# Turning the tiles of three passes on VectorE and by DMA instead of on TensorE

## The chip, the cores and the metric

The kernel runs on one core of a Trainium2 chip. The metric is the device time of one execution in microseconds. All arithmetic is in float32; the large products are made of three products each, of a high and a low part of both factors (`three`, lines 559 to 566).

## What is computed

The input x has 4 sequences of 512 tokens of width 512 (2048 tokens). Six steps are added to it in turn:

```
x = x + 0.5 * ffn0(layernorm(x))      ffn0: silu(x W1^T) * (x W3^T), Walsh-Hadamard, W2^T; hidden 2048
x = x + attention(layernorm(x))       normalised again, gamma and beta, causal softmax, plus residual
x = x + 0.5 * ffn0(layernorm(x))
x = x + 0.5 * ffn1(layernorm(x))      gate and up with ternary weights and scales, down; hidden 1408
x = x + state(layernorm(x))           tanh(x B^T) C^T + D * x; state 256
x = x + 0.5 * ffn1(layernorm(x))
```

## The kernel before

The instructions of each engine are written out by hand in program order; semaphores join the engines. x stays in SBUF, 16 tiles of 128 tokens. Each of the four ffn steps is done in two passes, one for each half of the tokens (a pair of sequences, 8 tiles): passes 0 and 1 are the first ffn0, 2 and 3 the second, 4 and 5 the first ffn1, 6 and 7 the second. Attention lies between passes 1 and 2, the state step between 5 and 6.

A pass is a loop over slots, one for each block of 128 hidden units: 16 slots of an ffn0 pass ("A") and 11 of an ffn1 pass ("B"). The up products of a slot are seven products on 128x512 tiles (p1, p5, p6, p2, then p7, p3, p4), a Strassen-Winograd scheme that works on 2x2 blocks: the half of the tokens and the half of the hidden units. PE's order in a slot is the first half (p1, p5, p6, p2), four down tiles of earlier slots (`down`, each into a bank of a ring of three PSUM banks; a bank is free again when VectorE has added it into x, line 2107), then the turns of that slot, then the second half (p7, p3, p4).

The products need the normalised tokens of a pass turned, with the features in the partitions. They are prepared ahead: pass 0 turns the tiles for pass 1, pass 2 for 3, 3 for 4, 4 for 5, 5 for the state step and 6 for 7; those of passes 0, 2 and 6 come from the opening, from attention and from the state step. Slots `norms` (5 to 8 in pass 0, 3 to 6 in passes 2 and 3): ScalarE normalises two tiles (`norm_pair`, line 1452) into `xn`. Slots `turn_slots`, one later: PE turns each of the two tiles by four transposes of 128x128 against an identity matrix (`turn_tiles`, `turn`, lines 997 and 855) into a bank of the same ring, and ScalarE copies the bank to `xs` (`turn_out`, line 1300). In the third-last and the second-last slot of a pass VectorE forms the sums of the scheme from `xs` (`sums`, line 2053), and in the last slot the high and low parts `xc_hi` and `xc_lo` for the next pass are made (`convert`, lines 1308 and 2072).

In a slot VectorE's order is `seed_z` (line 2136), the low part of the next weight block (pass 0 only, line 2091), the four adds, statistics in some slots, `sum_c22` (line 2145), the two gatings, then `hid_low` of token half 1 and of half 0 (line 2133), and in pass 0 the four sums of a raw weight block (line 2080). ScalarE makes the high parts in `hid_high` (line 1444), for half 0 after `seed_y` of the next slot.

All transfers are issued by SyncE's queue (SP) in program order. In pass 0 it stores the prepared weights (`w13_out`, `w2_out`) and fetches raw ones two blocks ahead. In later passes it loads, in the iteration of slot s, the up weights of slot s+1 (`w13_load`, line 579), which wait for p4 of slot s-1, and a down block (`w2_load`). There are two buffers of up weights and four of down weights.

## Time and profile before

| | |
|---|---|
| time, median of 3 runs | 1707.72 us (1706.44 to 1708.61) |
| profiled execution, span | 1703.6 us |
| PE busy | 1694.7 us, 99% |
| VectorE busy | 1154.4 us, 68% |
| ScalarE busy | 830.3 us, 49% |
| TensorE's granted clock, mean | 0.999 |
| moved by DMA | 344.56 MB, mean 202 GB/s |

The profile is of one execution, and its span runs from the first to the last instruction; no time of its own is given beside the span, so it stands next to the median of the timed runs, which is 4.1 us longer. Busy time of PE is the union of pipelined matmuls, so 99% says that it is never long without one.

### The profile page before, as it was taken

How to read it: one execution, taken by the hardware profiler on the slowest of the kernel's cores; microseconds unless marked ns; L12 is line 12 of the kernel's file. 1: busy time of each engine (PE TensorE's matmuls, PEld its weight loads, DVE VectorE, ACT ScalarE, POOL GpSimd, SP SyncE). 2: the span in 40 equal slices, each digit the busy share in tenths (PEclk: the TensorE clock that was granted, in tenths of full speed). 3: DMA queues.
4: the chain of work that ended last, by engine and by line, in shares of the span. 5: the costliest groups of instructions: out<-in, count | busy, mean ns of one | idle time of the engine just before them, and what ended most of it. 6: DMA issues, size and time to landing. Idle time of an engine off the chain costs nothing.

```text
span 1703.6 us, 21742 instructions
## 1 busy us (share of the span) xinstructions
PE 1694.7 (99%) x7707; PEld 1401.8 (82%) x7707; DVE 1154.4 (68%) x1808; ACT 830.3 (49%) x1359; POOL 125.5 (7%) x185
## 2 busy tenths in 40 slices
PE   9999999999999999999999999999999999999998
PEld 7788888888888888888888888888888888888887
DVE  8888678677775555754446554447768869877866
ACT  5745444465575543434223333224556556655644
POOL 1000000000012220000000000000000143200001
PEclk9999999999999999999999999999999999999999
DMA  9776665699985000253444433444666763366765
GB/s 317 266 310 247 229 258 211 236 377 369 369 333 207 1 0 1 87 191 126 153 167 167 167 142 136 167 167 146 232 215 211 273 222 112 113 242 234 257 221 213
DMA packets 97341, 344.56 MB, mean 202 GB/s; under 512 B 10192, under 2 KB 25424, under 8 KB 91856
## 3 DMA queue, kind: packets, MB, share of 16 engines
q1 hardware_dynamic: 97232, 343.14, 55.0%
q8 instruction: 65, 1.06, 0.2%
q14 instruction: 44, 0.36, 0.1%
HBM read 261.83 MB, written 81.26 MB: 201 GB/s over the span
## 4 chain that ended last, share of the span: by engine, by line
PE 94%; DVE 3%; DMA 1%; SPq 1%; issue 1%; ACT 0%; DVEq 0%; ACTq 0%
PE psum L561 35%; PE psum L563 30%; PE psum L565 27%; PE psum L857 2%; DMA x<-in_w2a 1%; SPq L705 1%; DVE xc_lo L2074 0%; DMA flat<-in_w3a 0%; DMA w<-w_kept 0%; PE psum L1134 0%; DVE att_lo L2043 0%; DVE fw_lo L2037 0%; SPq L664 0%; DVE x L2020 0%; DVE x L2123 0%
## 5 line engine op out<-in xcount | busy, mean ns | idle before, releaser
L561 PE MATMUL psum<-xc_hi,w 128*128 128x512 f32 x1544 | 604.6, 392 | 0.5 <-DVE psum L2143 0.3
L563 PE MATMUL psum<-xc_lo,w 128*128 128x512 f32 x1544 | 600.9, 389 | 0.0
L565 PE MATMUL psum<-xc_hi,w 128*128 128x512 f32 x928 | 361.3, 389 | 0.0
L561 PEld LDWEIGHTS psum<-xc_hi,w 128*128 128x128 f32 x1544 | 289.8, 188 | 64.4 <-DVE psum L2143 1.6
L563 PEld LDWEIGHTS psum<-xc_lo,w 128*128 128x128 f32 x1544 | 289.9, 188 | 58.8
L561 PE MATMUL psum<-w,hid 128*128 128x512 f32 x864 | 337.5, 391 | 0.0
L565 PE MATMUL psum<-w,hid 128*128 128x512 f32 x864 | 336.4, 389 | 0.0
L2107 DVE TENSOR_TENSOR x<-psum,x 128x512 f32<-128x512 f32 x256 | 173.0, 687 | 148.3 <-PE psum L565 147.7
L563 PE MATMUL psum<-w,hid 128*128 128x512 f32 x544 | 211.7, 389 | 0.0
L565 PEld LDWEIGHTS psum<-xc_hi,w 128*128 128x128 f32 x928 | 174.2, 188 | 36.7
L2131 DVE TENSOR_TENSOR hid<-sg,hid 128x512 fp32r<-128x512 f32 x212 | 144.3, 691 | 85.2 <-ACT hid L1450 83.3
L561 PEld LDWEIGHTS psum<-w,hid 128*128 128x128 f32 x864 | 162.2, 188 | 36.1 <-DVE x L2107 2.7
L565 PEld LDWEIGHTS psum<-w,hid 128*128 128x128 f32 x864 | 162.2, 188 | 33.9
L1480 ACT ACTIVATE psum<-psum 128x512 f32<-128x512 f32 x108 | 62.9, 582 | 237.6 <-PE psum L565 172.4
L1450 ACT ACTIVATE hid<-sg 128x512 fp32r<-128x512 f32 x204 | 125.6, 627 | 105.1 <-DVE sg L2156 51.9
L2147 DVE TENSOR_TENSOR sg<-psum,sg 128x512 f32<-128x512 f32 x104 | 71.6, 688 | 91.1 <-ACT psum L1480 90.7
L563 PEld LDWEIGHTS psum<-w,hid 128*128 128x128 f32 x544 | 102.2, 188 | 20.4
L2143 DVE TENSOR_TENSOR psum<-psum,sg 128x512 f32<-128x512 f32 x104 | 72.2, 694 | 43.8 <-PE psum L565 36.9
L1423 ACT ACTIVATE psum<-psum 128x512 f32<-128x512 f32 x108 | 62.8, 581 | 79.9 <-PE psum L565 54.7
L1884 POOL TENSOR_SCALAR var_eps<-meanvar 128x4 f32<-128x4 f32 x24 | 7.0, 290 | 1242.1 <-DVE meanvar L1988 865.1
L1472 ACT ACTIVATE sg<-psum 128x512 f32<-128x512 f32 x64 | 38.0, 593 | 89.2 <-PE psum L565 89.2
L1298 ACT ACTIVATE xn<-x,shift,rstd 128x512 f32<-128x512 f32 x88 | 65.7, 807 | 13.0 <-POOL shift L1887 9.9
(177 smaller groups left out, 2030.1 us busy)
## 6 DMA issues: line engine op xcount, KB each, us to landing
w<-w_kept SPq DMA_DIRECT2D x93, 896.0 KB, 6.6
w<-w_kept SPq DMA_DIRECT2D x130, 512.0 KB, 7.1
w<-w_kept SPq DMA_DIRECT2D x57, 640.0 KB, 4.4
w_kept<-w SPq DMA_DIRECT2D x16, 1792.0 KB, 7.3
w<-w_kept SPq DMA_DIRECT2D x93, 256.0 KB, 4.5
w_kept<-prep SPq DMA_DIRECT2D x12, 1792.0 KB, 7.6
w_kept<-w SPq DMA_DIRECT2D x16, 512.0 KB, 6.3
w_kept<-prep SPq DMA_DIRECT2D x12, 512.0 KB, 8.9
```

What stands on the lines that cost most here:

```text
L561: pe.matmul(out, a_hi, b_hi, start=start, stop=False, skip_group_check=onto)
L563: last = pe.matmul(out, a_hi, b_lo, start=False, stop=stop and zero == "a", skip_group_check=onto)
L565: last = pe.matmul(out, a_lo, b_hi, start=False, stop=stop, skip_group_check=onto)
L1298: return copy(out, x[:, i, :], AF.Identity, bias=shift[:, i:i + 1], scale=rstd[:, i:i + 1])
L1423: copy(bank(BY), bank(BX), AF.Copy).then_inc(y_seeded, 1)
L1450: copy(hid_of(u, c)[:, 0, :], own(u) if c else sg[:, 0, :], AF.Copy).then_inc(hid_hi_ready, 1)
L1472: copy(sg[:, 0, :], bank(BX), AF.Silu, scale=gate_scale(ps, s)).then_inc(c11_read, 1)
L1480: copy(bank(BW), bank(BY), AF.Copy).then_inc(w_seeded, 1)
L2107: tt(at_x, b, at_x, ALU.add).then_inc(added, 1)
L2131: tt(h[:, 1, :], source, h[:, 0, :], ALU.subtract).then_inc(hid_ready, 1)
L2143: tt(bank(BZ), bank(BY), own(u), ALU.add).then_inc(z_seeded, 1)
L2147: tt(own(u), bank(BY), own(u), ALU.add).then_inc(c22_ready, 1)
```

## The change

The turns of passes 0, 2 and 3 leave TensorE. In each `norms` slot of these passes ScalarE normalises two tiles into `xn[:, 0:2]`, each after VectorE has read the tile before in that buffer. VectorE then transposes each tile in 32x32 blocks into `swap` (a new use of the second half of `xn`), where the two tiles of a pair lie interleaved token by token. Four stores, one for each group of 32 partitions, write the pair to DRAM so that the blocks come in their new order, SP waits for them, and four loads bring it to `xs`. A piece that is contiguous in DRAM has 256 bytes in the stores and 1 KB in the loads. The tokens of passes 1, 3 and 4 then lie in pairs; `hid_high` and `hid_low` read them with a step of two and write the plain order. The other turns (for passes 0, 2, 5, 6, 7, the state step and attention) stay on TensorE. The blocks of `xs` are renumbered, and waits that counted turned tiles are counted anew.

```diff
@@ -75,6 +75,9 @@
 NORMS = {4: (3, 4, 5, 6), 5: (4, 5, 6, 7), 6: (4, 4, 5, 6), 7: ()}
 CONVERSIONS = {no: (3, 0, 2, 1, 4, 5, 6) if no == BEFORE_S else tuple(range(7)) for no in range(len(PASSES))}
+SWAPPED = (0, 2, 3)
+BLOCK = 32
+LANDED = 16 * 4
 FIRST_CONVERSION = {5: 6, 6: 5, 7: 6}
 TURNS = {4: (4, 5, 6, 7), 5: (5, 6, 7, 8), 6: (4, 5, 6, 7), 7: ()}
...
@@ -155,7 +163,7 @@
                         n = 2 * TURNED_EARLY.index(s) + j
                         self.bank["t", n] = b
                         ps.turns[s].append((n, n))
-            elif no < len(PASSES) - 1 and s in ps.turn_slots:
+            elif no < len(PASSES) - 1 and no not in SWAPPED and s in ps.turn_slots:
                 for j in range(2):
                     self.use(("n", self.turn), 3)
                     ps.turns[s].append((self.turn, 2 * ps.turn_slots.index(s) + j))
...
@@ -226,6 +235,7 @@
     w2_raw = nc.dram_tensor("w2_scratch", [HA // P, P, D], F32).ap()
     w13_kept = nc.dram_tensor("w13_kept", [W13_BASE["S"] + 1, P, 2 * 7 * 2 * P], F32).ap()
     w2_kept = nc.dram_tensor("w2_kept", [W2_BASE["S"] + 2, P, 2 * D], F32).ap()
+    turn_scratch = nc.dram_tensor("turn_scratch", [BLOCK, P // BLOCK, KD, P // BLOCK, 2 * BLOCK], F32).ap()
     mix_raw = nc.dram_tensor("mix_raw", [2, P, KD * D], F32).ap()
     mix_kept = nc.dram_tensor("mix_kept", [2, P, 2, KD * D], F32).ap()
...
@@ -254,9 +264,10 @@
         w2 = at("w2", [P, 4, 2, D], F32R, "w2")
         hid = at("hid", [P, 5, 2, TOK], F32R, "hid")
-        hid_more = [at(f"hid_more{i}", [P, 2, TOK], F32R, "xs", (4 + 8 * i) * KIB) for i in range(2)]
+        hid_more = [at(f"hid_more{i}", [P, 2, TOK], F32R, "xs", (8 + 4 * i) * KIB) for i in range(2)]
         sg = at("sg", [P, 3, TOK], F32, "sg")
         xn = at("xn", [P, 4, D], F32, "xn")
+        swap = at("swap", [P, P // BLOCK, KD, BLOCK, 2], F32, "xn", 4 * KIB)
         flat = at("flat", [P, 12, 2 * P], F32, "sp")
...
@@ -443,9 +457,31 @@
             return conv_base(no) + CONVERSIONS[no].index(m) + 1
-        def turns_before(no):
-            return PT * (no + 1 + (no >= BEFORE_S))
+        def all_turned(no):
+            if no - 1 in SWAPPED:
+                return turn_in[no - 1], PT // 2 * LANDED
+            return turned, PT * {0: 1, BEFORE_T: 2, BEFORE_S - 1: 3, BEFORE_S: 5, BEFORE_S + 1: 6}[no]
+        def swaps_before(ps):
+            return PT * SWAPPED.index(ps.no)
+        def paired(no):
+            return no - 1 in SWAPPED
+        def of_unit(u):
+            return next(ps.no for ps in passes if ps.u0 <= u < ps.u0 + ps.n)
+        def in_pairs(tile, no):
+            return tile.rearrange("p (h t i) -> p h i t", h=2, i=2) if paired(no) else tile
+        def by_tile(tile, no):
+            return tile.rearrange("p (h i t) -> p h i t", h=2, i=2) if paired(no) else tile
         def hid_of(u, c):
...
@@ -480,7 +516,7 @@
         def xs_cols(tile):
             c, i = tile // TT, tile % TT
-            return xs[:, c:c + 3:2, :, i * P:(i + 1) * P]
+            return xs[:, 2 * c:2 * c + 2, :, i * P:(i + 1) * P]
         def bank_tiles(b):
             return bank(b).rearrange("p (h k t) -> p h k t", h=2, k=2)
...
@@ -524,11 +560,11 @@
                 return score_ready, CH * TT
             return t_full, filled["v", CH - 1, 1]
-        sources = [xs[:, 0, :, :], xn[:, 0:2, :], xs[:, 4, :, :], xs[:, 2, :, :], xs[:, 1, :, :], xs[:, 3, :, :],
+        sources = [xs[:, 0, :, :], xn[:, 0:2, :], xs[:, 4, :, :], xs[:, 1, :, :], xs[:, 2, :, :], xs[:, 3, :, :],
                    xn[:, 2:4, :]]
         freeing = [p1_done, p5_done, p6_done, p2_done, p7_done, p3_done, p4_done]
-        s_sources = [xs[:, 0, :, :], xs[:, 2, :, :], xs[:, 1, :, :], xs[:, 3, :, :]]
+        s_sources = [xs[:, n, :, :] for n in range(4)]
         def s_blocks(c):
...
@@ -686,7 +722,10 @@
             def mix_raw_load(r):
                 sp.wait_ge(mix_stored[r // 2], 16)
-                sp.wait_ge(turn_ready, PT if r < 2 else 2 * PT)
+                if r < 2:
+                    sp.wait_ge(turn_ready, PT)
+                else:
+                    sp.wait_ge(*all_turned(1))
                 if r:
                     sp.wait_ge(mix_split_kept, 16 * r)
                 sp.dma_start(mix_in_raw[:, :, :].rearrange("p k d -> p (k d)"),
...
@@ -704,6 +743,23 @@
                     sp.wait_ge(fw_out, 4 * s + j + 1)
                     sp.dma_start(w2_raw[4 * j:4 * j + 4, :, s * P:(s + 1) * P].rearrange("b p d -> p b d"),
                                  stage_of(s, j).rearrange("p (b d) -> p b d", b=4)).then_inc(scratch_done[j], 16)
+            def turn_load(ps, k):
+                c, cols = k // 2, slice(k % 2 * 2 * P, (k % 2 + 1) * 2 * P)
+                sp.wait_ge(swapped, swaps_before(ps) + 2 * k + 2)
+                if k:
+                    sp.wait_ge(turn_in[ps.no], k * LANDED)
+                elif SWAPPED.index(ps.no):
+                    sp.wait_ge(*all_turned(SWAPPED[SWAPPED.index(ps.no) - 1] + 1))
+                for a in range(P // BLOCK):
+                    sp.dma_start(turn_scratch[:, :, :, a, :].rearrange("i b k t -> i (b k) t"),
+                                 swap[a * BLOCK:(a + 1) * BLOCK, :, :, :, :].rearrange("p b k j i -> p (b k) (j i)")
+                                 ).then_inc(turn_stored[ps.no], 16)
+                sp.wait_ge(turn_stored[ps.no], (k + 1) * LANDED)
+                for b in range(P // BLOCK):
+                    sp.dma_start(xs[b * BLOCK:(b + 1) * BLOCK, 2 * c:2 * c + 2, :, cols].rearrange("p h k t -> p (h k) t"),
+                                 turn_scratch[:, b, :, :, :].rearrange("i k a t -> i k (a t)")).then_inc(turn_in[ps.no], 16)
             rows_in(0)
             sp.dma_start(had_raw[:, :], t["hadamard"]).then_inc(had_in, 16)
...
@@ -753,6 +809,8 @@
                 w2_out(s)
                 if s in MIX_IN:
                     mix_split_out(MIX_IN.index(s))
+                if s in passes[0].norms:
+                    turn_load(passes[0], passes[0].norms.index(s))
                 if s + 1 in MIX_IN:
                     mix_raw_load(MIX_IN.index(s + 1))
...
@@ -785,6 +843,8 @@
                         w2_load(ps.w2_0 + s, W2_BASE[ps.kind] + s)
                     if early and not late_low:
                         w13_low_load(ps.v0 + s + 1, W13_BASE[ps.kind] + s + 1)
+                    if ps.no in SWAPPED and s in ps.norms:
+                        turn_load(ps, ps.norms.index(s))
                     if ps.no == 1:
                         if s == 0:
                             sp.dma_start(half_down_s[:, :], t["down_s"]).then_inc(hds_in, 16)
...
@@ -1446,11 +1506,21 @@
                 if u == 0:
                     act.wait_ge(mix_stored[1], 16)
                 if plan.hid_set[u, c] >= 5:
-                    act.wait_ge(xc_ready, conv_base(next(ps.no for ps in passes if ps.u0 <= u < ps.u0 + ps.n)) + 7)
-                copy(hid_of(u, c)[:, 0, :], own(u) if c else sg[:, 0, :], AF.Copy).then_inc(hid_hi_ready, 1)
+                    act.wait_ge(xc_ready, conv_base(of_unit(u)) + 7)
+                no = of_unit(u)
+                copy(by_tile(hid_of(u, c)[:, 0, :], no), in_pairs(own(u) if c else sg[:, 0, :], no),
+                     AF.Copy).then_inc(hid_hi_ready, 1)
             def norm_pair(ps, k):
+                if ps.no in SWAPPED:
+                    for tile in (2 * k, 2 * k + 1):
+                        if k:
+                            act.wait_ge(swapped, swaps_before(ps) + tile - 1)
+                        else:
+                            act.wait_ge(xc_ready, conv_base(ps.no) + 7)
+                        normalise(norm_event(ps) + tile // TT, tile % TT, xn[:, tile % 2, :]).then_inc(xn_ready, 1)
+                    return
                 first = [n for r in ps.turns for n, _ in r][0]
                 for tile in (2 * k, 2 * k + 1):
                     if tile >= TT:
@@ -1531,11 +1601,6 @@
                     if ps.no == 0 and s == ps.norms[0]:
                         act.wait_ge(mix_split_kept, 32)
                     norm_pair(ps, ps.norms.index(s))
-                if ps.no != BEFORE_T - 1:
-                    for n, tile in ps.turns[s]:
-                        if tile == 0:
-                            act.wait_ge(xc_ready, conv_base(ps.no) + 7)
-                        turn_out(n, tile, plan.bank["n", n])
                 seed_w(u)
                 if last and following:
                     convert(following, 2)
...
@@ -2052,9 +2117,9 @@
             def sums(ps, step):
-                b11, b12, b21, b22, t2 = (xs[:, n, :, :] for n in range(5))
+                b11, b21, b12, b22, t2 = (xs[:, n, :, :] for n in range(5))
                 if step == 0:
-                    dve.wait_ge(turned, turns_before(ps.no))
+                    dve.wait_ge(*all_turned(ps.no))
                     tt(b12, b22, b12, ALU.subtract).then_inc(sums_ready, 1)
                 elif step == 1:
                     dve.wait_ge(sums_ready, 4 * ps.no + 1)
...
@@ -2077,6 +2142,15 @@
                 dve.wait_ge(xc_hi_ready, conv_base(BEFORE_S) - 4 + m + 1)
                 tt(xc_lo[:, m, :, :], s_sources[m], xc_hi[:, m, :, :], ALU.subtract).then_inc(xc_ready, 1)
+            def swap_pair(ps, k):
+                for j in range(2):
+                    dve.wait_ge(xn_ready, plan.norm_base[ps.no] + 2 * k + j + 1)
+                    if k:
+                        dve.wait_ge(turn_stored[ps.no], k * LANDED)
+                    nc.vector.transpose(swap[:, :, :, :, j], xn[:, j, :].rearrange("p (k b t) -> p b k t", k=KD, b=P // BLOCK)
+                                        ).then_inc(swapped, 1)
             def w13_sums(n):
                 dve.wait_ge(*raw_landed(n))
...
@@ -2126,12 +2200,13 @@
                 for _, i, d in ps.downs[ps.n][TT * half:TT * (half + 1)]:
                     finish_tile(ps, i, d)
-            def low(key, h, source):
+            def low(key, h, source, no):
                 dve.wait_ge(hid_hi_ready, plan.lo_no[key])
-                tt(h[:, 1, :], source, h[:, 0, :], ALU.subtract).then_inc(hid_ready, 1)
+                tt(by_tile(h[:, 1, :], no), in_pairs(source, no), by_tile(h[:, 0, :], no),
+                   ALU.subtract).then_inc(hid_ready, 1)
             def hid_low(u, c):
-                low((u, c), hid_of(u, c), own(u) if c else sg[:, 0, :])
+                low((u, c), hid_of(u, c), own(u) if c else sg[:, 0, :], of_unit(u))
             def seed_z(u):
                 dve.wait_ge(p6_done, u + 1)
...
@@ -2238,6 +2313,9 @@
                 if following and s in (ps.n - 3, ps.n - 2):
                     for step in range(2):
                         sums(following, 2 * (s - ps.n + 3) + step)
+                swapping = ps.no in SWAPPED and s in ps.norms
+                if swapping and ps.no:
+                    swap_pair(ps, ps.norms.index(s))
                 if not last:
                     sum_c22(u)
                     if preparing and s == 1:
@@ -2247,6 +2325,8 @@
                         w2_split(0)
                         w2_split(1)
                     hid_low(u, 1)
+                    if swapping and ps.no == 0:
+                        swap_pair(ps, ps.norms.index(s))
                     hid_low(u, 0)
                 if ps.no == 0 and s != 1 and s + 2 < UNITS["A"]:
                     w13_sums(s + 2)
```

## Rows read from the trace of the kernel before

**Rows 1.** The page, parts 1 and 4: engines over the span; chain that ended last.

```profile
PE 1694.7 (99%) x7707; PEld 1401.8 (82%) x7707; DVE 1154.4 (68%) x1808; ACT 830.3 (49%) x1359; POOL 125.5 (7%) x185
...
PE 94%; DVE 3%; DMA 1%; SPq 1%; issue 1%; ACT 0%; DVEq 0%; ACTq 0%
```

**Rows 2.** Waits of PE (total us, times, longest), first and last of four.

```profile
PE psum L1233 <- POOL warm L1861: 1.3, 1, 1.3
...
PE psum L561 <- DVE psum L2143: 0.3, 1, 0.3
```

**Rows 3.** Timeline of ScalarE in pass 0: start, length, one copy per slot.

```profile
126.06 0.58 ACT L1480 ACTIVATE psum<-psum 128x512 f32<-128x512 f32 x1 [4.76 <-PE psum L565]
...
141.07 0.58 ACT L1480 ACTIVATE psum<-psum 128x512 f32<-128x512 f32 x1 [0.17 <-PE psum L565]
...
156.99 0.58 ACT L1480 ACTIVATE psum<-psum 128x512 f32<-128x512 f32 x1 [0.68 <-PE psum L565]
```

**Rows 4.** The same timeline in pass 2.

```profile
740.81 0.58 ACT L1480 ACTIVATE psum<-psum 128x512 f32<-128x512 f32 x1 [6.20 <-PE psum L565]
...
755.77 0.58 ACT L1480 ACTIVATE psum<-psum 128x512 f32<-128x512 f32 x1 [4.80 <-PE psum L565]
...
771.62 0.58 ACT L1480 ACTIVATE psum<-psum 128x512 f32<-128x512 f32 x1 [0.67 <-PE psum L565]
```

**Rows 5.** Groups by form: busy us, mean ns of one, idle before.

```profile
L1985 DVE BATCH_NORM_STATS2 stats<-x 128x6 f32<-128x512 f32 x72 | 45.2, 678 | 0.1
...
L857 PE MATMUL psum<-ident,xn 128*128 128x128 f32 x320 | 41.6, 273 | 0.2
...
L2074 DVE TENSOR_TENSOR xc_lo<-xn,xc_hi 128x1024 fp32r<-128x1024 f32 x16 | 19.5, 1217 | 1.8 <-ACT xc_hi L1329 1.8
...
L2009 DVE TENSOR_SCALAR y<-x,rstd,shift 128x512 f32<-128x512 f32 x4 | 1.9, 542 | 1.5 <-POOL shift L1887 1.5
```

**Rows 6.** Timeline of VectorE in pass 0, from one slot into the next.

```profile
160.41 0.69 DVE L2131 TENSOR_TENSOR hid<-sg,hid 128x512 fp32r<-128x512 f32 x1
162.24 0.69 DVE L2131 TENSOR_TENSOR hid<-sg,hid 128x512 fp32r<-128x512 f32 x1 [1.15 <-ACT hid L1450]
...
164.10 0.42 DVE L2089 TENSOR_TENSOR flat<-flat 128x256 f32<-128x256 f32 x1
...
166.29 2.02 DVE L2094 TENSOR_TENSOR w<-flat,w 128x1792 fp32r<-128x1792 f32 x1 [1.16 <-ACT w L1352]
```

**Rows 7.** Timeline of ScalarE in the same slot.

```profile
164.55 1.70 ACT L1352 ACTIVATE w<-flat 128x1792 fp32r<-128x1792 f32 x1 [1.51 <-DVE flat L2089]
```

**Rows 8.** Timeline of the weight loads (PEld) in the same slot.

```profile
168.97 0.19 PEld L561 LDWEIGHTS psum<-w,hid 128*128 128x128 f32 x1 [0.18 <-DVE x L2107]
```

**Rows 9.** Timeline of VectorE in pass 2, slot 3.

```profile
753.77 1.33 DVE L2107 TENSOR_TENSOR x<-psum,x 128x512 f32<-128x512 f32 x2
756.38 0.69 DVE L2147 TENSOR_TENSOR sg<-psum,sg 128x512 f32<-128x512 f32 x1 [1.28 <-ACT psum L1480]
757.76 0.69 DVE L2156 SCALAR_TENSOR_TENSOR sg<-sg 128x512 f32<-128x512 f32 x1 [0.69 <-ACT sg L1489]
```

**Rows 10.** Timeline of SyncE's queue in pass 2 at the start of slot 4.

```profile
758.48 0.80 SPq L577 DMA_DIRECT2D w<-w_kept  x2
759.32 0.43 SPq L609 DMA_DIRECT2D w<-w_kept  x1
```

**Rows 11.** DMA issues: count, KB each, median us from issue to landing.

```profile
w<-w_kept SPq DMA_DIRECT2D x93, 896.0 KB, 6.6
...
w_scratch<-stage SPq DMA_DIRECT2D x8, 256.0 KB, 7.4
...
w_scratch<-x SPq DMA_DIRECT2D x4, 256.0 KB, 2.3
```

**Rows 12.** The instructions of one tensor: ns min/median/max of SyncE's issue.

```profile
L705 SPq DMA_DIRECT2D w_scratch<-x x4: 359/359/418, 67.9 to 73.6; - x4
```

**Rows 13.** Timeline of VectorE in pass 1, first add of a slot.

```profile
394.88 0.69 DVE L2107 TENSOR_TENSOR x<-psum,x 128x512 f32<-128x512 f32 x1 [1.40 <-PE psum L565]
```

More of the change, by code:

```diff
@@ L110, in __init__ @@
         self.own, self.other, self.spare = [], [], 2
-        self.turn = PT
+        self.turn = self.norm = PT
+        self.norm_base = {}
         for no in range(len(PASSES)):
@@ L114, in __init__ @@
                 self.turn += PT
+                self.norm += PT
                 self.downs_before_t = self.d
@@ L131, in add_pass @@
         self.passes.append(ps)
+        if no not in (BEFORE_T - 1, len(PASSES) - 1):
+            self.norm_base[no] = self.norm
+            self.norm += PT
         tiles = {s: [] for s in range(ps.n + 1)}
@@ L193, in state_space @@
         self.s_unit, self.s_w2 = self.u, self.w2
-        self.s_downs, self.s_turn = [[] for _ in range(CH)], self.turn
+        self.s_downs, self.s_turn, self.s_norm = [[] for _ in range(CH)], self.turn, self.norm
+        self.norm += PT
         self.uses += -self.uses % 4
@@ L362, in build @@
         mix_in = [sem(f"mix_in{m}") for m in range(2)]
+        turn_stored = {no: sem(f"turn_stored{no}") for no in SWAPPED}
+        turn_in = {no: sem(f"turn_in{no}") for no in SWAPPED}
         out_done = sem("out_done")
@@ L1004, in turn_tiles @@
                         bank_free("n", n)
-                        pe.wait_ge(xn_ready, n + 1)
+                        pe.wait_ge(xn_ready, plan.norm_base[ps.no] + tile + 1)
                         turn(xn[:, tile % 4, :], plan.bank["n", n]).then_inc(turn_ready, 1)
@@ L1310, in convert @@
                 if ps.no == BEFORE_S and m in (0, 3):
-                    act.wait_ge(turned, turns_before(ps.no) - TT)
+                    act.wait_ge(turned, all_turned(ps.no)[1] - TT)
                 elif m in (0, 3, 4, 5):
-                    act.wait_ge(turned, turns_before(ps.no))
+                    act.wait_ge(*all_turned(ps.no))
                 if m and (ps.no, m) != (BEFORE_S, 3):
@@ L1331, in state_convert @@
             def state_convert(m):
-                act.wait_ge(turned, turns_before(BEFORE_S) - PT)
+                act.wait_ge(turned, all_turned(BEFORE_S)[1] - PT)
                 act.wait_ge(freeing[m], S_UNIT)
@@ L1749, in s_norm @@
                     else:
[L1750 removed]
+                        act.wait_ge(turn_ready, PT + i + 1)
                     normalise(2 * CH + c, i, xn[:, i, :]).then_inc(xn_ready, 1)
@@ L2398, in state_low @@
             def state_low(c, j):
-                low(("s", c, j), hid[:, 2 * (c % 2) + j, :, :], sg[:, j, :])
+                low(("s", c, j), hid[:, 2 * (c % 2) + j, :, :], sg[:, j, :], BEFORE_S)
             def state_x_low(c, i):
@@ L2458, in state_space @@
                 state_term(1)
-                dve.wait_ge(xn_ready, plan.s_turn + TT)
+                dve.wait_ge(xn_ready, plan.s_norm + TT)
                 for i in range(TT):
@@ L2520, in s_turn @@
             def s_turn(c, h):
-                b, n = t_use["s", c, h] % 2 * 2, 2 * PT + TT * c + 2 * h
+                b, n = t_use["s", c, h] % 2 * 2, PT + TT * c + 2 * h
                 dve.wait_ge(turn_ready, n + 2)
```

4 lines of the change are left out of this document (2 added, 2 removed).

## The prediction, made before the result was known

> **What bounds the kernel now.** I read four views in this order. The page first: PE (TensorE's matmuls) is busy in 99% of the 1703.6 us span, VectorE in 68%, ScalarE in 49%, and the chain that ended last is 94% PE [rows 1]. Then PE's waits: four entries, together 3.0 us [rows 2]. So hardly anything can be gained by shortening a wait; a gain must come from work that leaves PE, and each microsecond by which another engine or a transfer makes PE wait is lost in full. Third, a regular mark in each slot: ScalarE's copy of line 1480 runs right after product p7, once per slot. In pass 0 it stands at 126.06, 141.07 and 156.99: a slot without a turn takes 15.01 us, one in which PE turns two tiles takes 15.92 us [rows 3]. In pass 2 it is 14.96 and 15.85 us [rows 4]. Last, VectorE, ScalarE and the queues in one slot of pass 0 and of pass 2 [rows 6 to 12], to see what slack the new work has.
>
> **What it removes from PE.** In passes 0, 2 and 3 four slots each have eight transposes (two tiles by four column blocks). The price of such a slot is the difference of periods: 15.92 - 15.01 = 0.91 us in pass 0 [rows 3] and 15.85 - 14.96 = 0.89 us in pass 2 [rows 4]; pass 3 repeats pass 2 and the four slots of a pass agree within 0.02 us. The sum is 4 x 0.91 + 8 x 0.89 = 10.8 us. The group row gives a second reading: 320 transposes cover 41.6 us, 0.13 us each [rows 5], so 96 cover 12.5 us; this counts the pipelined end of each group, which overlaps the next matmul, so I take 10.8 and keep 12.5 for the low end. The mean of 273 ns in that row is a latency and not what a transpose costs. ScalarE loses 24 copies out of PSUM; it had slack, I count 0. The three-bank ring sees 24 uses less, a multiple of 3 and of 4, so later passes keep their banks.
>
> **What it adds on VectorE.** 24 transposes 128x512 in 32x32 blocks, two per slot in 12 slots. The trace of before has none. Bounds from the nearest rows: 542 ns (tensor_scalar, SBUF to SBUF, same elements) and 1217 ns (twice the elements) [rows 5]. I take 680 ns, the one-input statistics of the same 512 elements (678) [rows 5], as it is nearest in shape; back to back such instructions follow each other about 0.61 us apart (160.41 plus 0.61 is where the next could start).
>
> The Trainium skill (Vector Engine (DVE) Microarchitecture Reference, section 3.8) says that the transpose array sustains one element per cycle and lane. No run here shows it. Its figure of 311 ns for 128x128 (VectorE: DVE Perf Modes, The three transpose paths) would make an estimate of about 0.7 us for 512 columns, with the same sum.
>
> Pass 0 has the tight place. There the two transposes stand between hid_low(u,1) and hid_low(u,0), and behind them on VectorE are hid_low(u,0), the four weight sums, seed_z, the weight split and the adds into x. The first of these adds frees the PSUM bank that PE's fourth down tile needs. In the trace: hid_low(u,1) starts at 160.41, hid_low(u,0) at 162.24 after 1.15 us of waiting for ScalarE, the sums end at 164.52, ScalarE splits from 164.55 to 166.25, VectorE from 166.29 [rows 6, 7], and the weight load of the fourth tile waits 0.18 us for the add, until 168.97 [rows 8]. PE still runs without a gap, so this chain has no slack left: what delays hid_low(u,0) delays PE. Two transposes can start at 161.02 and hid_low(u,0) at 160.41 + 3 x 0.61 = 162.24, its present time; at 0.65 us apart it would be 0.1 us later. I take 0.1 us for each of four slots, 0.4 us; with 1217 ns each, hid_low(u,0) starts at about 161.1 + 2.4 = 163.5, 1.2 us late, 4.9 us in all.
>
> In passes 2 and 3 the transposes stand before sum_c22. VectorE is free at 755.10, sum_c22 starts at 756.38 after waiting 1.28 us for ScalarE, and behind it lies another 0.69 us of waiting [rows 9]. Two transposes take 1.3 us: 0. With 1217 ns the delay is 1.1 us, of which 0.7 disappears in the next wait and the rest before PE's next slot; also 0.
>
> **The strided reads.** In passes 1, 3 and 4 hid_high and hid_low read every second float, as the tokens lie in pairs. No row has such a read. From below 0; from above I let each instruction take the cost of its elements twice, +0.6 us. Then pass 1 suffers most, in its 11 slots with weight preparation: the chain to the first add gets two VectorE and one ScalarE instruction longer, 1.8 us, against 1.40 us of waiting before that add [rows 13], so 0.4 us x 11 = 4.4 us. I take 0: the elements and their count stay as they are and each partition still reads one float at a time.
>
> **What it adds on SyncE's queue and the DMA engines.** Per pair four stores (2048 pieces of 256 bytes) and four loads (512 of 1 KB), in order on SP: it waits for the transposes, issues four stores, waits for them to land, issues four loads. Behind them on this queue stand the next weight loads, which PE needs at its next slot but one. Pass 2, slot 3: transposes done at 756.4 [rows 9]; an issue takes 0.36 to 0.42 us [rows 12], four 1.6 us. A scattered store of 256 KB lands after 2.3 us [rows 11], so stores to landing are about 1.6 + 2.3 = 3.9 us, and the four load issues 1.6 more: SP is free at 761.9 and not at 758.48, 3.4 us late. The weight loads need from first issue (758.48) to the last landing (issue 759.32 [rows 10] plus 6.6 [rows 11]) 7.4 us, plus at most 1.6 us behind the turned tiles: 770.9. Slot 5 starts at 758.3 + 14.96 = 773.3. There are 2.4 us to spare, cost 0. From above: 7.4 us to land, as the same kind of store took while the opening loads ran [rows 11]; then SP is free at 767.0, weights are in at 776.0, 2.7 us late in each of eight slots, 21.6 us. I take the lower one, since the slot's own weight loads were issued a period before 758.48, at 743.5, and by their 7.4 us have landed at 751. In pass 0 SP waits at each step for VectorE, and the raw weights it fetches are used more than a slot later: 0. The turned tiles are first used in the last slots of the pass, five or more slots on: 0.
>
> The Trainium skill (DMA: Bandwidth & Descriptors, Specifications) says that pieces under 512 bytes are read, modified and written, below line rate. That speaks against these stores; by it they take perhaps twice the engine time, and it is one more reason to keep the SP case below.
>
> **Sum.** -10.8 + 0.4 = -10.4 us. The profiled span would go from 1703.6 to 1693.2 us. The median of the timed runs, 1707.72, is 4.1 us above that span; what lies outside the span does not change, so I predict 1697.3 us.
>
> **Rivals.**
> - The transposes run at half rate: 1217 ns, +4.9 us in pass 0 as above, time 1701.8. For it: no row of this operation. Against: the one-input forms of [rows 5] take 0.54 and 0.68 us for 512 elements.
> - The strided reads run at half rate: +4.4 us, time 1701.3; with the first together 1706.2, no change. For it: nothing but the lack of a row.
> - The other side: SP's queue is held. One mechanism: the wait for the stores keeps the weight loads of passes 2 and 3 back, and PE starts slots 5 to 8 late. It begins to hurt when the stores need over 2.3 + 2.4 = 4.7 us to land, and eats the whole gain at 1.3 us per slot more (10.4 / 8), at 6.0 us. At 7.4 us: 1697.3 + 21.6 = 1718.9. For it: the two other kinds of [rows 11] take 6.6 and 7.4 us. Against: the store in 512-byte pieces at 2.3 us.
> - It does less than it says: something else sets the length of a slot, and it does not shrink to 14.96. Against: in every pass the slots before and after the turns run at that period, so nothing else sets it.
>
> **Chances.** Forecast (gain of 8 to 12 us) 0.71; transposes slow 0.08; strided reads slow 0.06; queue held 0.11, of which 0.02 ends near no change; not as it says or something unseen, 0.04. For 8 in 10: the low end is 1694.5 (12.5 us gone and 0.7 us of spread between runs), the high end 1704 (either half-rate case and a little of the queue case). 0.2% is 3.4 us, about what can be told from no change here. Faster 0.83 (forecast, most of both half-rate cases), the same 0.07, slower 0.10 (the queue case, and the unseen).
>
> **What would show it.** PE 96 transposes less; the line 1480 copies of passes 0, 2 and 3 at 15.0 us throughout, slots 4 to 7 of passes 2 and 3 included. VectorE: 24 new instructions, near 0.68 us. In pass 0 the weight load of the fourth down tile shows how late the add is: 0.18 us idle before it means that the forecast holds, over 1 us that the first rival does. hid instructions of passes 1, 3 and 4 at 0.63 and 0.69 us, or near 1.2. SP: weight loads of passes 2 and 3 some 3.4 us later than before, and PE waiting for w or not. The prediction is wrong if PE waits more than 2 us on w<-w_kept, or if the sum of PE's waits grows by more than 3 us.

## The result, and the profile after

The changed kernel takes 1695.34 us (median of four runs, 1693.49 to 1697.35); the kernel before, run beside it, 1707.08 us (1705.11 to 1708.61, four runs). The ratio is 0.9936, 95% interval 0.9924 to 0.9948: 11.7 us faster. Predicted were 1697.3 us and 1694.5 to 1704.0. A later repeat (below) gave 1695.86 against 1706.51, 10.7 us. The profiled execution spans 1693.8 us, before 1703.6; TensorE's mean granted clock is 0.999 in both.

The page of the changed kernel, part 1 (busy time, share of the span, instructions), answers to [rows 1]:

```profile
PE 1684.5 (99%) x7611; PEld 1392.2 (82%) x7611; DVE 1169.8 (69%) x1832; ACT 820.1 (48%) x1335; POOL 125.7 (7%) x185
```

PE has 96 instructions less and 10.2 us less to do, VectorE 24 and 15.4 us more. PE's waits (total us, times, longest; a fifth of 0.2 us has no releaser), against the 3.0 us of [rows 2]:

```profile
PE psum L1293 <- POOL warm L1926: 1.3, 1, 1.3
PE psum L597 <- DMA w<-w_kept: 1.0, 1, 1.0
PE psum L886 <- DVE fw_lo L2102: 0.7, 1, 0.7
PE psum L597 <- DVE psum L2218: 0.5, 2, 0.3
```

The wait for w<-w_kept lies after 1300 us, in pass 5, which the change does not touch; its slot takes 7.64 us where the kernel before has 6.34. It is absent in the repeat. The mark once per slot, line 1550 now, in pass 0 and in pass 2 (ScalarE's timeline: start, length, in brackets the idle time before it and what ended it):

```profile
125.43 0.58 ACT L1550 ACTIVATE psum<-psum 128x512 f32<-128x512 f32 x1 [4.76 <-PE psum L601]
140.17 1.52 ACT L1358 ACTIVATE xn<-x,shift,rstd 128x512 f32<-128x512 f32 x2 [4.22 <-DMA mix_kept<-mix_prep]
141.60 0.58 ACT L1550 ACTIVATE psum<-psum 128x512 f32<-128x512 f32 x1
156.24 0.58 ACT L1550 ACTIVATE psum<-psum 128x512 f32<-128x512 f32 x1 [3.37 <-PE psum L601]
...
752.28 0.58 ACT L1550 ACTIVATE psum<-psum 128x512 f32<-128x512 f32 x1 [4.80 <-PE psum L601]
767.24 0.58 ACT L1550 ACTIVATE psum<-psum 128x512 f32<-128x512 f32 x1 [4.80 <-PE psum L601]
```

In pass 2 every slot takes 14.96 us, those that had a turn too (15.85 in [rows 4]); pass 3 is the same. In pass 0 three of the four former turn slots take 15.02 to 15.04 us (15.92 in [rows 3]). The slot ahead of the first, from 125.43, takes 16.17 us and the first itself 14.64, together 0.8 us more than two plain slots: ScalarE's first norm stands behind a wait for the store of mix_prep, and the mark behind the norm. This wait exists in the kernel before too (3.07 us there, 4.22 here). It changes from run to run: in the eight other runs below that leave these two slots as they are, the two together take 30.1 to 30.7 us, against 30.8 here and 30.0 for two plain ones.

By the marks the five slots of pass 0 gave 2.8 us (78.7 to 75.9) and passes 2 and 3 together 7.3. The rest of the 9.8 us between the two spans is not the change: 0.6 us shorter before pass 0's first norm, 1.3 lost in the slot of pass 5 above, 0.4 that one slot of pass 6 took longer in the execution before.

VectorE's group, and its timeline in slot 3 of pass 2, against [rows 5] and [rows 9]:

```profile
L2151 DVE STREAM_TRANSPOSE swap<-xn 128x512 f32<-128x512 f32 x24 | 15.6, 686 | 0.0
```

```profile
750.29 1.33 DVE L2181 TENSOR_TENSOR x<-psum,x 128x512 f32<-128x512 f32 x2
751.53 1.29 DVE L2151 STREAM_TRANSPOSE swap<-xn 128x512 f32<-128x512 f32 x2
752.90 0.69 DVE L2222 TENSOR_TENSOR sg<-psum,sg 128x512 f32<-128x512 f32 x1
754.27 0.69 DVE L2231 SCALAR_TENSOR_TENSOR sg<-sg 128x512 f32<-128x512 f32 x1 [0.69 <-ACT sg L1559]
```

The transposes fill the gap of 1.28 us; behind them VectorE still waits 0.69 us for ScalarE, as before. The tight place of pass 0, against [rows 6] and [rows 8] (VectorE, then PEld):

```profile
160.31 1.30 DVE L2151 STREAM_TRANSPOSE swap<-xn 128x512 f32<-128x512 f32 x2
161.53 0.65 DVE L2205 TENSOR_TENSOR hid<-sg,hid 128x512 fp32r<-128x512 f32 x1
...
165.54 2.03 DVE L2168 TENSOR_TENSOR w<-flat,w 128x1792 fp32r<-128x1792 f32 x1 [1.16 <-ACT w L1412]
```

```profile
168.22 0.19 PEld L597 LDWEIGHTS psum<-w,hid 128*128 128x128 f32 x1 [0.20 <-DVE x L2181]
```

SP's queue in the same slot of pass 2, and its landings, against [rows 10] and [rows 11]:

```profile
752.85 3.45 SPq L756 DMA_DIRECT2D turn_scratch<-swap  x4
758.14 1.75 SPq L761 DMA_DIRECT2D xs<-turn_scratch  x4
759.93 0.90 SPq L613 DMA_DIRECT2D w<-w_kept  x2
```

```profile
turn_scratch<-swap SPq DMA_DIRECT2D x48, 128.0 KB, 2.5
```

The first weight load stands 7.65 us behind the mark of its slot (759.93 - 752.28), before 2.71 (758.48 - 755.77): 4.9 us late. This is the first pair of the pass; behind the other three the weights are 4.1 us late. PE did not wait for them.

### The profile page after: what moved, and what is told of

It is laid out like the page before. It is cut to its first block, busy times and chain, and to the rows that moved or that the text cites. A ratio compares the mean times of both kernels' runs of the same rounds, so it can differ in the third digit from the quotient of the medians.

```text
span 1693.8 us, 21648 instructions
## 1 busy us (share of the span) xinstructions
PE 1684.5 (99%) x7611; PEld 1392.2 (82%) x7611; DVE 1169.8 (69%) x1832; ACT 820.1 (48%) x1335; POOL 125.7 (7%) x185
## 3 DMA queue, kind: packets, MB, share of 16 engines
q8 instruction: 64, 1.05, 0.2%
## 4 chain that ended last, share of the span: by engine, by line
PE 92%; DVE 3%; DMA 2%; SPq 1%; issue 1%; ACT 0%; ACTq 0%; DVEq 0%
PE psum L597 34%; PE psum L599 30%; PE psum L601 26%; PE psum L917 2%; DMA x<-in_w2a 1%; DMA mix_kept<-mix_prep 1%; SPq L744 1%; DVE xc_lo L2139 0%; DMA flat<-in_w3a 0%; DMA w<-w_kept 0%; DMA mix_in_raw<-mix_raw 0%; DVE att_lo L2108 0%; PE psum L1194 0%; DVE fw_lo L2102 0%; SPq L700 0%
## 5 line engine op out<-in xcount | busy, mean ns | idle before, releaser
L599 PEld LDWEIGHTS psum<-w,hid 128*128 128x128 f32 x544 | 102.2, 188 | 20.6
```

Source lines behind the costliest of these rows:

```text
L599: last = pe.matmul(out, a_hi, b_lo, start=False, stop=stop and zero == "a", skip_group_check=onto)
```

## The experiments

Times are medians, beside runs of the kernel before on the same chip.

**1. Pass 0 alone, and passes 2 and 3 alone.**

```diff
-SWAPPED = (0, 2, 3)
+SWAPPED = (0,)        # first run
+SWAPPED = (2, 3)      # second run
```

> Only pass 0 is turned by VectorE and DMA; passes 2 and 3 keep their turns on TensorE. Theory (the gain is TensorE's removed transposes slot by slot, and nothing else): 4 slots x 0.91 us less 0.1 us each for the late add, 3.2 us below the kernel before, about 1703.9 us; the marks after p7 in slots 6 to 9 of pass 0 are 15.0 us apart, those in passes 2 and 3 stay at 15.85. Rival (a good part of the gain comes from something that all three passes share, such as ScalarE's missing copies or the ring of banks): the gain is not a third of that of the full change, under 1 us or over 6.

> Only passes 2 and 3 are turned by VectorE and DMA. Theory: 8 slots x 0.89 us, 7.1 us below the kernel before, about 1700.0 us, with no new wait of TensorE; together with the run of pass 0 alone it makes up the whole change. Rival (the added work in pass 0 costs more than its turns were worth): this kernel is as fast as the full change, 1695.3 us, or faster.

Pass 0 alone: 1703.25 against 1706.57 us, ratio 0.9977 (0.9967 to 0.9987), a gain of 3.3 us. Passes 2 and 3 alone: 1699.74, ratio 0.9955 (0.9938 to 0.9971), 6.8 us. Together 10.1, of the whole's 10.7 to 11.7: the two parts add up. In the first the turn slots of passes 2 and 3 keep their 15.86 us, in the second those of pass 0 their 15.91. No run takes away the transposes and leaves ScalarE's 24 copies; that the gain is TensorE's work is read from the kernel before, in which PE has no wait at all in the turn slots, and from PE's busy time, 10.2 us less.

**2. Each tile transposed twice.** The same tile into the same buffer, one behind the other.

```diff
-nc.vector.transpose(swap[..., j], xn[:, j, :]...).then_inc(swapped, 1)
+for last in (False, True):
+    turned_one = nc.vector.transpose(swap[..., j], xn[:, j, :]...)
+    if not last: link(turned_one)
+turned_one.then_inc(swapped, 1)
```

> As the changed kernel, but VectorE transposes each tile twice in a row. Theory (in pass 0 the chain from hid_low to the first add has no slack, in passes 2 and 3 the wait for ScalarE covers it): two more transposes a slot, 1.4 us, appear in full in four slots of pass 0 and not in passes 2 and 3: 5.6 us above the changed kernel, about 1700.9 us; the weight load of the fourth down tile waits about 1.6 us in those slots. Rival (VectorE is idle for a quarter of pass 0, that covers it): no change, 1695.3 us. Second rival (no slack in passes 2 and 3 either): 12 x 1.4, 1712 us.

1702.39 us (1699.77 to 1705.74, ten runs), ratio 0.9975 (0.9965 to 0.9984); the span is 6.4 us over the changed kernel's. VectorE in pass 0, and PE's waits:

```profile
161.68 2.80 DVE L2152 STREAM_TRANSPOSE swap<-xn 128x512 f32<-128x512 f32 x4
164.40 0.65 DVE L2209 TENSOR_TENSOR hid<-sg,hid 128x512 fp32r<-128x512 f32 x1
```

```profile
PE psum L597 <- DVE x L2185: 4.9, 4, 1.3
```

Four transposes take 2.8 us, 1.5 more than two. In pass 0 the slots with them take 16.07, 16.54, 16.44 and 16.46 us against 14.64, 15.02, 15.04 and 15.03, 5.8 us in all, and PE waits there four times, up to 1.3 us, for the add. The former turn slots of passes 2 and 3 stay at 14.96. So the chain that the prediction named has no slack in pass 0, and in the other two passes 1.5 us more of VectorE costs nothing.

**3. The stores doubled and tripled.** Each pair's four stores go to two or three scratch tensors, and SP waits for all of them; only one is read.

```diff
-for a in range(P // BLOCK):
-    sp.dma_start(turn_scratch[:, :, :, a, :]..., swap[...]...)
-sp.wait_ge(turn_stored[ps.no], (k + 1) * LANDED)
+for r in range(3):                              # 2 in the other run
+    for a in range(P // BLOCK):
+        sp.dma_start(turn_scratches[r][:, :, :, a, :]..., swap[...]...)
+sp.wait_ge(turn_stored[ps.no], (k + 1) * LANDED * 3)
```

> As the changed kernel, but each pair is stored three times (to three tensors in DRAM) before SyncE's queue goes on. Theory (SP held back costs nothing until the weights come late): 8 more stores of 0.65 us issue each, 5.2 us more hold; in passes 2 and 3 the weights, issued from 759.9, would be issued from 765.1 and be in at about 772.7, 2.8 to 3.8 us after the start of slot 5 at 769.9; in eight slots 22 to 30 us, 1717 to 1725 us, with TensorE waiting for w<-w_kept in slots 5 to 8 of passes 2 and 3 and nowhere in pass 0. Rival (the hold is hidden with much room): within 1 us of 1695.3.

> Each pair's four stores are issued twice, to two scratch tensors (the second copy is not read), and SP waits for all eight before the loads; the transposes and all else are the changed kernel's. By the run with three copies SP's weight loads then come some 3.4 us later than in the changed kernel (twelve stores held them back 6.8 us more). Theory (the prediction's margin of 2.4 us behind a delay of 3.4, of which 0.9 is left at the measured delay of 4.9): slots of passes 2 and 3 that took 22.1 and 20.2 us with three copies take 18.7 and 16.8, the others 15.0, so some 5.5 us a pass, 11 in all, 1706 (1703 to 1709), and in pass 0 nothing or up to 1 us. Rival (the ring of weight buffers gives more margin than I gave it, so that only a hold longer than a slot costs): 1695 to 1697, all slots of passes 2 and 3 at 14.96.

Three times: 1739.87 us, ratio 1.0188 (1.0171 to 1.0205), much more than expected. SP's queue in pass 2, PE's waits, and two stretches behind the mark at 783.42 (us, busy us and instructions of PE, PEld, VectorE, ScalarE and GpSimd, then PE's granted clock, DMA share, GB/s):

```profile
769.03 9.35 SPq L759 DMA_DIRECT2D turn_scratch<-swap  x12
780.21 1.75 SPq L764 DMA_DIRECT2D xs<-turn_scratch  x4
782.00 0.90 SPq L615 DMA_DIRECT2D w<-w_kept  x2
```

```profile
PE psum L599 <- DMA w<-w_kept: 22.2, 10, 5.0
PE psum L599 <- DVE x L2184: 6.6, 2, 4.9
PE psum L599 <- ACT psum L1486: 4.7, 1, 4.7
```

```profile
783.42:788.00 4.58, 2.68 (x12) 1.88 (x10) 3.22 (x5) 1.81 (x3) 0.11 (x1) 1.00 0.96 357
788.00:793.00 5.00, 1.87 (x5) 1.51 (x6) 0.00 (x0) 0.00 (x0) 0.00 (x0) 0.52 0.90 253
```

The slots of pass 2 take 22.1, 16.5, 20.2 and 15.8 us, and passes 2 and 3 lose 29.7 us, the upper end of what was expected. Of these PE waited only 20.1 us. Most of the rest goes with the clock: after PE had waited 5.0 us, its granted clock was 0.52 in the stretch from 788 to 793, near the lower of its two levels (1.2 and not 2.4 GHz), and its matmuls began 0.43 us apart instead of 0.23 until 794.7. In the eight slots 33 matmuls begin so far apart, 6.5 us in all. The other 15 us are lost in pass 0, where I had expected nothing (slots of 17.0, 21.5 and 21.9 us): SP is held 16.4 to 17.1 us by three of the four pairs there, longer than a slot of 15.0, and the raw weights that it fetches for the split stand behind.

Twice: 1703.57 us (1697.75 to 1705.53, ten runs), ratio 0.9981 (0.9972 to 0.9991), 8.2 us over the changed kernel, inside the 1703 to 1709 expected. The profiled execution (1697.75 us) was the fastest of the ten, so its slots show only about 2 of the 8 us, and where the others lost the rest is not known:

```profile
767.01 5.64 SPq L759 DMA_DIRECT2D turn_scratch<-swap  x8
774.45 1.75 SPq L764 DMA_DIRECT2D xs<-turn_scratch  x4
776.24 0.91 SPq L615 DMA_DIRECT2D w<-w_kept  x2
```

```profile
PE psum L599 <- DMA w<-w_kept: 1.9, 5, 0.7
```

These weight loads stand 9.8 us behind the mark at 766.44, 7.1 us later than in the kernel before. Weights are needed a slot later, and so each delay belongs to the loss of the slot behind: in pass 2 the four delays are 7.5, 7.1, 6.9 and 6.8 us and the losses 0.95, 0.47, 0.65 and 0.15. With 4.9 us nothing is lost. So in this execution PE begins to wait at a delay between 6.2 and 6.7 us (each delay less its loss).

**4. The norms and turns of pass 0 one slot later**, against the 0.8 us found at 140 us, and beside it the changed kernel once more.

```diff
-self.norms = NORMS.get(no, tuple(range(self.offset + 3, self.offset + 3 + PT // 2)))
+first = self.offset + 3 + (no == 0)
+self.norms = NORMS.get(no, tuple(range(first, first + PT // 2)))
```

> As the changed kernel, with the normalising and transposing of pass 0 one slot later (slots 6 to 9), so that ScalarE no longer comes to its wait for the mix_kept store just after that store was issued. Theory (the landing of that store stalls TensorE in slot 5 by 0.2 to 1.2 us, in part given back in slot 6): 0.5 to 1.0 us faster than the changed kernel, about 1694.6 us, slot 5 at 15.0 us, and a smaller spread of the runs. Rival (the wait is hidden and slot 5 is long for another reason): no change, slot 5 stays long.

> The changed kernel once more, as the partner of the other runs of this call on the same chip. Theory and rival alike: 0.9936 of the kernel before, 10 to 12 us below it; the profile has slot 5 of pass 0 at 15.0 to 16.2 us, since ScalarE waits there for the mix_kept store, whose landing varies.

Shifted: 1696.61 us (1695.08 to 1697.3), not faster than the repeat's 1695.86 (1695.06 to 1697.56, ratio 0.9936, 0.9922 to 0.995). The stall at 140 us shrinks (two slots of 15.44 and 15.01 us against 16.04 and 14.64, 0.2 us; this is within what the two slots vary by from run to run), and a new one comes at the other end, where the slot from 216.66 takes 16.40 us (SP, then ScalarE):

```profile
206.98 2.63 SPq L757 DMA_DIRECT2D turn_scratch<-swap  x4
211.66 1.75 SPq L762 DMA_DIRECT2D xs<-turn_scratch  x4
215.75 0.34 SPq L732 DMA_DIRECT2D mix_in_raw<-mix_raw  x1
```

```profile
220.63 1.06 ACT L1353 ACTIVATE mix_prep<-mix_in_raw 128x1024 fp32r<-128x1024 f32 x1 [2.02 <-DMA mix_in_raw<-mix_raw]
```

The load of mix_raw must wait until the last pair's turned tiles have landed, and so it is issued at 215.75 and not, as in the changed kernel, at 202.93. It is the rival of the held queue in another form, at a price of 1.4 us, in the one place where SP has a transfer due in the same slot.

**5. Pass 4 turned by VectorE too.** First with SP's stores and loads of pass 4 one slot late; then with the norm shift and the same lateness in passes 2 and 3 as well.

```diff
-SWAPPED = (0, 2, 3)
+SWAPPED = (0, 2, 3, 4)
+LATE_TURNS = (4,)     # (2, 3, 4) in the second run
-if ps.no in SWAPPED and s in ps.norms:
-    turn_load(ps, ps.norms.index(s))
+if ps.no in SWAPPED and s - (ps.no in LATE_TURNS) in ps.norms:
+    turn_load(ps, ps.norms.index(s - (ps.no in LATE_TURNS)))
```

> As the changed kernel, and pass 4 too is turned by VectorE and DMA, with its stores and loads issued one slot later on SyncE's queue, after the weight loads of that slot. Theory (what counts is TensorE's removed work as long as the wait for ScalarE covers VectorE and the weights are not held back): four slots of 10.88 us become 9.98 us, 3.6 us faster than the changed kernel, about 1691.7 us. Rival (slots of 10 us are too short to hide a hold of 7 us on SyncE's queue): TensorE waits for w<-w_kept in slots 5 to 9 of pass 4 by 2 us each, and it is 4 us slower than the changed kernel or more.

> Both edits together, and the stores and loads of passes 2 and 3 also issued one slot later, after the weight loads. Theory: the two gains add, 4.3 us faster than the changed kernel, about 1691.0 us; in passes 2 and 3 the weight loads are issued at the slot's start again, but this brings no time since they were not late. Rival (issuing behind the weight loads is what matters): a further 1 us or more in passes 2 and 3.

1706.88 us (ratio 0.9999, 0.999 to 1.0008) and 1708.59 (1.0013, 1.0003 to 1.0022): the whole gain is gone. In the second all slots of passes 2 and 3 stay at 14.96 us, so the lateness is harmless there. The loss is in five slots of pass 4, which take 11.79, 16.63, 11.88, 15.15 and 10.95 us in the first run where the changed kernel has 12.68, 10.88, 10.89, 10.87 and 10.00: 11.1 us. VectorE of the first run shows why:

```profile
1233.44 1.31 DVE L2158 STREAM_TRANSPOSE swap<-xn 128x512 f32<-128x512 f32 x2 [5.95 <-DMA turn_scratch<-swap]
```

There is one swap buffer; the stores of the pair before had been issued only at 1227.24, a slot late, and VectorE stood for them with its chain for PE behind it.

**6. Pass 4 with SP's steps put elsewhere.** First the stores in their own slot and the loads behind the next slot's weights; then both between a slot's first weight load and the wait in front of the others; last the same with a scratch tensor for each pair.

```diff
+if ps.no == APART and s - 1 in ps.norms:       # first run, ahead of w2_load
+    turn_load(ps, ps.norms.index(s - 1))
...
+for step, ps, k in between:                    # second run, in w13_load
+    step(ps, k)
 sp.wait_ge(p4_done, v - 1)
...
+turn_scratch = turn_scratches[k if ps.no == APART else 0]   # third run
-if k:
+if k and ps.no != APART:
     sp.wait_ge(turn_in[ps.no], k * LANDED)
```

> Pass 4 is turned by VectorE as well, as in the run with four turned passes, but SP's work is put apart there: the four stores of a pair stand behind the slot's ordinary weight loads and ahead of its low weights, so that they are issued in the slot of the transposes, and the pair's four loads stand one slot later, behind that slot's first weight loads, so that SP does not stand and wait for the stores to land. Theory (the four-pass run lost 11 us because I had issued the stores of pass 4 a slot late, so that VectorE, with one swap buffer, stood 2.8 to 6.0 us in front of the next pair's transposes until the stores had landed): these idle times go, TensorE's slots 4 to 7 of pass 4 take 9.97 to 10.0 us where the changed kernel has 10.88, and the whole comes to 1691.7 (four slots by 0.9 us under 1695.3), 1691 to 1693. Rival 1 (VectorE is the bound of these 10.9 us slots once 1.3 us of transposes stand in them): no store is waited for, but the slots take 10.4 to 10.9 us, 1693.5 to 1695.5. Rival 2 (the SP queue: weights land late whatever the order): waits for w<-w_kept of over 2 us in pass 4 and 1697 or more.

> Four turned passes again (0, 2, 3 and 4). In pass 4 both steps of a pair now stand in the one stretch in which SP has nothing to issue: between a slot's first weight load and the wait for TensorE in front of the two others. There the loads of the pair before come first and then the stores of this pair. What the two runs before showed: with stores and loads a slot late VectorE stood 2.8 to 6.0 us for the swap buffer; with the loads right behind a slot's weights they landed after 7.3 us (2.6 us in the changed kernel), the next pair's stores waited for them, SP came late to the weights behind, and one slot took 21.8 us. Theory (all of the loss was in where SP's steps stand, none in the transposes): xs<-turn_scratch lands before the next pair is turned, no wait for w<-w_kept or for turn_scratch over 1 us in pass 4, its slots from the fourth on take 11.8, 10.0, 10.0, 10.0 us where the changed kernel has 12.7, 10.9, 10.9, 10.9, and the whole comes to 1691.7 us, 1690.5 to 1693.5. Rival 1 (VectorE binds a 10 us slot with 1.3 us of transposes in it): slots of 10.3 to 10.9 us, 1693 to 1696. Rival 2 (SP has no room in a slot of 10 us for eight more DMAs, 4.4 us of issue, wherever they stand): waits for w<-w_kept of 2 us or more, 1698 or more.

> As the run before (four turned passes, pass 4's loads and then stores between a slot's first weight load and the wait in front of the others), with one more thing: each of pass 4's four pairs has a scratch tensor in DRAM of its own, so that a pair's stores no longer wait until the loads of the pair before have landed. The run before showed no wait of VectorE and slots of 9.98 us where nothing was late, but xs<-turn_scratch landed after 8.5 us behind the weights on SP's queue, the next stores waited 3.7 us and more for it, and the weights behind came late (7.1 us in one wait, slots of 23.9 and 27.1 us). Theory (the reuse of one scratch tensor was the link by which late loads held back SP): the stores are issued at the transposes' end, the two later weight loads at the times of the changed kernel, no wait for w<-w_kept over 1 us in pass 4, its slots from the fourth on take 11.8, 10.0, 10.0, 10.0 us, and the whole comes to 1691.7 us, 1690.5 to 1694. Rival (1 MB more on SP's queue in these four slots fills it: 2.9 MB in 10 us are 290 GB/s of the 400 that the best slices show): weights still land over 1 us late and the time is 1696 or more.

All three failed: 1709.68 us (ratio 1.0019, 1.0009 to 1.003), 1724.77 (1.0107, 1.009 to 1.0124) and 1715.0 (1.0051, 1.0035 to 1.0068). VectorE is not what binds: in the second and third its waits for turn_scratch are gone, and slots with a turn but without a late weight take 9.97 us, as hoped. What is late are weights. Waits of PE in the third, and in the first the landing of the loads (us, min/median/max; the changed kernel has 2.3/2.6/4.6):

```profile
PE psum L600 <- DMA w<-w_kept: 16.7, 7, 5.1
```

```profile
DMA to landing us min/median/max: 6.4/7.3/9.3
```

A late weight costs more than PE's wait here too. In the second run PE waits 21.4 us for w<-w_kept, and pass 4 is 27.4 us longer than in the changed kernel instead of 3.6 shorter. That is 31.0 us for 21.4; in pass 4 some 40 matmuls begin 0.43 us apart, 8.0 us in all. After the first wait, of 2.35 us, they begin 0.23 us apart until 1231.4 and then 0.43 us until 1234.7.

Why no order helped may be seen in the time that the queue's packets took, as a share of 16 engines. The view is the DMA view of a stretch of whole slots: four slots of pass 2 before (755.77 to 819.5 us), the same four after (752.28 to 812.12), three slots of pass 4 after (1226.58 to 1259.22), and in the third run the same three slots of pass 4 (1226.5 to 1279.4), which take 22.1, 10.0 and 20.6 us there. Columns: packets, MB, share.

```profile
q1 hardware_dynamic: 2304, 9.44, 40.2%
```

```profile
q1 hardware_dynamic: 13053, 13.63, 71.4%
```

```profile
q1 hardware_dynamic: 2380, 7.90, 66.7%
```

```profile
q1 hardware_dynamic: 11181, 11.68, 81.7%
```

In passes 2 and 3 the weights of a slot take 63.7 x 0.402 / 4 = 6.4 us of all 16 engines; with a pair it is 59.8 x 0.714 / 4 = 10.7 us. A pair costs 4.3 us for 1.05 MB, 245 GB/s, where the weights move at 9.44 MB / 25.6 us = 369 GB/s. A slot of 14.96 us has room for 10.7. In pass 4 the weights alone take 32.6 x 0.667 / 3 = 7.3 us of a slot; by this estimate 7.3 + 4.3 = 11.6 us do not fit into 10.9, still less into the 10.0 that the saved turns should leave. My expectation for the last run had set 2.9 MB a slot against 400 GB/s; it is 7.90 / 3 + 1.05 = 3.7 MB, and the small pieces run at the lower rate besides.

That the engines' time is what binds pass 4 is not shown. For it: in the third run the share is 1.00 to 1.08 from 1226 to 1232, around PE's first wait. Against it as the whole cause: the same bytes in the second and third run end 10 us apart, so the order on the queue counts as well, and the engines stand idle (share 0.00) from 1245.0 to 1248.9, while PE catches up and the queue waits for it. The packets' time is not a fixed price either: in the third run it is 52.9 x 0.817 / 3 = 14.4 us a slot, and a share can exceed 1. Larger pieces, which would test it, were not tried.

## Why the prediction was right

- **What PE loses, -10.8 us.** Right: eleven of the twelve turn slots went to the period of their neighbours (14.96 and 15.03 us); the twelfth is one of the two that the stall at 140 us mixes. The two parts alone gave 3.3 and 6.8 us against terms of 3.2 (with the 0.4) and 7.1. The other reading, 12.5 us from the group row, counted pipelined ends, as the prediction said.
- **The transposes, 680 ns.** Measured 686 ns, 1.29 us for two. The Trainium skill (Vector Engine (DVE) Microarchitecture Reference, section 3.8) gives one element per cycle and lane for the transpose array; 686 ns for 512 columns, and the nearly equal 678 ns of the one-input statistics in [rows 5], agree. The distance of 0.61 us between two instructions does not come out of the row that the prediction names for it (there VectorE is busy from 160.41 to 162.24 - 1.15 = 161.09), but it is what the trace now shows: VectorE's instructions in pass 0 start at 159.70, at 160.31 and, two further on, at 161.53.
- **The chain of pass 0, +0.4 us.** Right in place, too high in size: the weight load waits 0.20 us where it waited 0.18, and the slots are 0.02 us longer, 0.1 us in all. The doubled transposes show that the place is as tight as described, and its price: 1.5 us more of VectorE (2.80 against 1.30) made these slots 1.4 to 1.5 us longer.
- **The strided reads, 0.** Right for the time. VectorE's hid instructions did not change; ScalarE's pay 34 ns (628 to 662 ns in passes 1 and 3), a twentieth of the upper bound. The slots of pass 3, which has these reads, stay at 14.96 us, and in pass 1, where the prediction had seen the danger, eleven slots take 166.1 us (336.96 to 503.07) against 166.2 before (340.27 to 506.49).
- **SP's queue, 0.** The verdict held, two numbers under it did not. A store's issue takes 634 ns (561 to 1444), not 0.36 to 0.42, so that the first pair of pass 2 held the queue 7.1 us and not 5.5, and the next 6.2; the weights came 4.9 and 4.1 us late instead of 3.4. The margin that I had worked out, 3.4 + 2.4 = 5.8 us, was a little short: the doubled stores put it at 6.2 to 6.7. Of it 1.3 to 1.8 us are left behind the first pair of a pass and 2.1 or more behind the others, where the prediction had 2.4. The price of this rival, taken as the lateness alone (21.6 us), would have been too low: with the stores tripled PE waited 20.1 us and passes 2 and 3 lost 29.7, as the granted clock was lower after the waits.
- **Not in the sum.** The 0.8 us at 140 us in pass 0. By the marks the three passes gave 10.1 us of the 10.4; that the span, 1693.8, comes so near to 1693.2 is partly luck, as the three differences outside them (0.6 and 0.4 us shorter, 1.3 longer) nearly cancel. And the step from span to median: I had taken 4.1 us as fixed, but only 1.8 us of it lie outside the span (1695.64 for 1693.8; the runs of the kernel before on record have 1.8 to 1.9 too); the rest is spread between runs: the profiled execution of the kernel before was one of the shorter ones. So 1697.3 came out 2 us too high while the predicted difference of 10.4 is close to the 10.7 and 11.7 measured.
- **The small pieces.** The Trainium skill (DMA: Bandwidth & Descriptors, Specifications) puts pieces under 512 bytes below line rate. The trace agrees: a pair, half of whose bytes go in pieces of 256 bytes and half in 1 KB, has 245 GB/s against 369. What share of that is due to the 256-byte pieces was not measured. It did not move this result, as the engines had 4.3 us of a slot free; it may be part of what closes pass 4.

## What to carry to other kernels

When PE is busy in 99% of the span, price a move off PE by the difference of two periods of one regular mark, with and without the work, and not by the mean of its instructions. Before moving data through DRAM instead, add up the DMA engines' time of one slot (share x length) with the new packets at the rate that pieces of their size reach, and compare it with the shortest slot: here 10.7 of 14.96 us cost nothing, and with an estimated 11.6 of 10.9 every order tried lost more than all that was gained. A transfer that must be waited for on an in-order queue is priced by what is queued behind it, and moving it to another slot only changes what that is. When it does make TensorE wait for microseconds, the loss is larger than the wait (29.7 us for 20.1 here), because the granted clock was at its lower level for some microseconds afterwards.

## What the hardware showed unexpectedly

- Issuing a store of 128 KB in 512 pieces of 256 bytes takes 0.63 us on SP's queue, the matching load in pieces of 1 KB 0.43 us.
- ScalarE pays 34 ns for reading 512 floats at a step of two; VectorE pays nothing measurable (692 to 693 ns).
- The same load lands after 2.6 us when it is issued ahead of a slot's weights and after 7.3 us behind them.
- After a wait of PE of 2.35 us its matmuls ran 1.3 us at 0.23 us apart and then 3.3 us at 0.43 us apart; after one of 5.0 us they ran at 0.43 us at once, for 3.6 us.
